# Two graph-attention layers, 16 groups in a software pipeline: next group's statistics and the first attention's tiles set elsewhere in the order

## Chip, cores and metric

One core of a Trainium2 chip. The time is device microseconds of one execution. The kernel before takes 1215.11 us (median of 3 runs, 1213.73 to 1215.54).

## The reference, cut to what matters

`x` is 128 graphs of 64 nodes with 384 features, `adj` a boolean 64x64 matrix for each graph. Two residual layers:

```python
h = relu(layernorm(x))
# layer 0: 12 heads of 32, additive attention
v  = einsum('bnd,ade->bane', h, W); th = tanh(v)
s  = th @ w_src + (th @ w_dst)^T;   s = leaky(s, 0.2); s = where(adj, s, -999)
y  = elu(softmax(s) @ v + b);       g = sigmoid(h @ H_w.T + H_b)
x  = x + g * y + (1 - g) * h
h = relu(layernorm(x))
# layer 1: 6 heads of 64, dot-product attention
q, k, v = h @ Wq + bq, h @ Wk + bk, h @ Wv + bv
x  = x + softmax(q k^T / 8 + mask(adj)) @ v @ Wf + bf
```

## The kernel before, in words

A group is 8 graphs, 512 token rows, held as 4 tiles of 128 rows (`TILES`); there are 16 groups. Nothing of the loop runs on the host: `iterations` writes out 17 rounds, i = 0 to 16. In round i the engines do layer 0 of group i, layer 1 of group j = i - 1, and prepare the normalised input of group i + 1 (`norm0`, `inv_std(0, i + 1)`, `normalise0`, `turn_h0`, `h0_parts`, `h0_lows`). Each engine has its own written order, and semaphores with constant counts tie them together. There is no other scheduler. A dense product in fp32 is made as three products of a high and a low part (`product`, L611 to L613), so a left operand is turned by TensorE into PSUM, copied by ScalarE as the high part, and VectorE makes the low part from the same PSUM bank.

TensorE's order in a round, with the names used below:

- head: four tiles of values (W0) and gate (Hw) of layer 0; then the turns of `th` (L597), of the layer-1 input `p1` (L597), and the small product for source and destination scores (L691), up to the first `Wq` product.
- middle: Q, the layer-0 score blocks (L679), K, V, the masks (L727), the layer-1 scores (L741).
- tail: the turns of the next h0 (`turn_h0`), the turns of the layer-0 probabilities (`turn_probs`, 6 banks), `attend0` of a pair of tiles twice (L775), the turns of the layer-1 probabilities, `attend1` twice (L793), the turns of the layer-1 result (L597, `attn1_low`), and the `Wf` product.

VectorE in the head: `values0(0)` (adds the bias to the first value tile, L911), then `norm0(i + 1)` (four BATCH_NORM_STATS L823 and four BATCH_NORM_AGGREGATE L828, behind a wait for the load of x), then `values0(1)`, the mask, `values0(2)`, `values0(3)`, `hT1l` (L988), the blocks of destination scores (L993); then `softmax0` of four tiles (from L959). In the tail: maxima and differences of the layer-1 scores (L946, L948), `mask1` (L1010), `h0_lows` (L839), `divide0` of four tiles (L888, L890), `divide1` of four (L899, L901), `close(0)`, and the low part of the layer-1 result (L1024), which the `Wf` product waits for.

ScalarE takes `values0_made` of a tile before its tanh (L459), and does `normalise1` (L420, four tiles) between the tanh of tile 1 and that of tile 2. POOL computes the reciprocal deviations (`inv_std`, L364 to L372), adds to x, and waits for VectorE's `gated`. SP loads x of group i + 2 once the store of group j has landed.

PSUM has 8 banks, used in a ring. `RING` lists the 64 uses of a round in order, `job(name, k)` is a use's place, its bank is the place modulo 8, and `take` makes TensorE wait for the reader of the use 8 places before. So a change of TensorE's order changes which reader frees which bank.

Of the kernel before, what the change touches and what calls it, by code (L numbers as in the profile page):

```python
# [8 lines left out]
ALU = mybir.AluOpType  # L9
# [6 lines left out]
P = 128  # L16
# [15 lines left out]
def two_layer_gnn(nc, x, adj, W0, b0, w_src, w_dst, H_w, H_b, Wq, bq, Wk, bk, Wv, bv, Wf, bf, out, d_scratch):  # L32
# [5 lines left out]
    with ExitStack() as ctx:  # L38
# [181 lines left out]
        def jobs(name, layer, signal, n):  # L220
# [14 lines left out]
            + jobs("values1_made", 1, values1_made, 4)  # L235
            + jobs("scores1_shifted", 1, scores1_shifted, 4)
            + jobs("h0_low", NEXT, h0_low, 3)
            + jobs("probs0T_copied", 0, probs0T_copied, 6)
            + jobs("attn0_made", 0, attn0_made, 4)
            + jobs("probs1T_copied", 1, probs1T_copied, 3)  # L240
            + jobs("attn1_made", 1, attn1_made, 4)
            + jobs("attn1_low", 1, attn1_low, 3)
            + jobs("out_made", 1, out_made, 4)
# [4 lines left out]
        def job(name, k):  # L248
            return place[name, k]

        def last_reader(i, at):
# [27 lines left out]
        def _(sp):  # L279
# [28 lines left out]
            def body(i, par):  # L308
                j = i - 1
                if real(i + 1):  # L310
                    load_adj(i + 1, 1 - par)
                if i == 0:
                    load_x(2)
                if real(i):
                    sp.wait_ge(values0_made, TILES * (i + 1))
                    if real(j):
                        sp.wait_ge(attn0_full, 2 * i)
                    else:
                        sp.wait_ge(ones_made, 3)
                    for g in range(2):  # L320
                        for o in range(2):
                            sp.dma_start(V0[64 * o:64 * o + 64, g, o].rearrange("p t k e -> p (t k) e")[:, :, 0:E0],
                                         v_tok[64 * g:64 * g + 64].rearrange("p t (k o e) -> p (t k) o e", o=2, e=E0)[:, :, o])\
                                .then_inc(values0_spread, 16)
                if real(j):
                    sp.wait_ge(values1_made, TILES * (j + 1))
                    if real(j - 1):
                        sp.wait_ge(attn1_full, 2 * j)
                    for g in range(2):
                        for o in range(2):  # L330
                            sp.dma_start(V1[64 * o:64 * o + 64, g].rearrange("p t k e -> p (t k) e")[:, :, 0:E1],
                                         v_tok[64 * g:64 * g + 64].rearrange("p t (k o e) -> p (t k) o e", o=2, e=E1)[:, :, o])\
                                .then_inc(values1_spread, 16)
                if real(j):
                    sp.wait_ge(out_made, (j + 1) * TILES)
                    sp.dma_start(out_v[j], x_in[:, j % 3]).then_inc(out_stored, 16)
                    if real(i + 2):
                        sp.wait_ge(out_stored, 16 * (j + 1))
                        load_x(i + 2)
# [6 lines left out]
        def _(pool):  # L346
# [36 lines left out]
            def body(i, par):  # L383
                j = i - 1
                if real(j):
                    inv_std(1, j)
                if real(i + 1):
                    inv_std(0, i + 1)
                if real(j):
# [3 lines left out]
                if real(i):  # L393
                    pool.wait_ge(h0_made, TILES * (i + 1))
                    for t in range(TILES):
                        pool.tensor_tensor(x_in[:, i % 3, t], x_in[:, i % 3, t], h0[:, par, t], ALU.add).then_inc(x_plus_h, 1)  # L396
                    pool.wait_ge(x_plus_h, TILES * (i + 1))
                    for t in range(TILES):
                        pool.wait_ge(gated, TILES * i + t + 1)
                        pool.tensor_tensor(x_in[:, i % 3, t], x_in[:, i % 3, t], ee[:, t], ALU.subtract).then_inc(x2_made, 1)  # L400
# [5 lines left out]
        def _(act):  # L406
# [27 lines left out]
            for c in range(C):  # L434
                act.activation(wh["Hw"][:, c, :], ps[:, 1 + c, 0:D], ACT.Copy).then_inc(w_high, 1)
            act.wait_ge(w_loaded["W0"], 16 * C)
# [14 lines left out]
            def body(i, par):  # L451
# [13 lines left out]
                def copy_q(c):  # L465
                    if real(j):
                        if c == 0 and real(j - 1):
                            act.wait_ge(scores1_full, 2 * j)
                        if c == 0 and real(i - 1):
                            act.wait_ge(attn0_full, 2 * i)  # L470
                        act.wait_ge(q_full, C * j + c + 1)
# [45 lines left out]
                if real(i):  # L517
                    if real(j):
                        act.wait_ge(attn0_full, 2 * i)
                    else:  # L520
                        act.wait_ge(w_low, C)
# [9 lines left out]
                if real(i):  # L531
# [7 lines left out]
                    act.activation(src_rows[:], sd, ACT.Identity, scale=is_dst_src[:, 1:2], bias=is_dst_src[:, 0:1]).then_inc(srcdst_copied, 1)  # L539
                if real(i + 1):  # L540
                    normalise0(i + 1, 1 - par)
                copy_q(0)
# [5 lines left out]
                leaky(3)  # L548
                exp0(0)
                if real(i):  # L550
                    for t in range(TILES):
# [7 lines left out]
                exp0(3)  # L559
                if real(i + 1):  # L560
                    h0_parts(i + 1)
                if real(i):
# [13 lines left out]
                exp1(3)  # L576
                exp_elu(0)
                exp_elu(1)
                if real(j):
                    for c in range(3):  # L580
                        act.wait_ge(probs1_turned, 3 * j + c + 1)
                        act.activation(KT[:, c], ps[:, job("probs1T_copied", c) % BANKS], ACT.Copy).then_inc(probs1T_copied, 1)
                exp_elu(2)
                exp_elu(3)
                if real(j):
                    act.wait_ge(values1_full, TILES * (j + 1))
                    for c in range(C):
                        act.wait_ge(attn1_turned, C * j + c + 1)
                        act.activation(hT1h[:, c], ps[:, job("attn1_low", c) % BANKS], ACT.Copy).then_inc(attn1_high, 1)

            iterations(act, body)
# [3 lines left out]
        def _(pe):  # L595
# [23 lines left out]
            for c in range(C):  # L619
                for f in range(C):  # L620
                    mm = turn(ps[:, 1 + c, f * P:(f + 1) * P], staged["Hw"][:, f, c * P:(c + 1) * P])
                mm.then_inc(hw_turned, 1)
# [20 lines left out]
            def body(i, par):  # L643
# [119 lines left out]

                def attend0(pair):

                    pe.wait_ge(values0_spread, 64 * (i + 1))
                    pe.wait_ge(probs0T_copied, 6 * i + 3 * pair + 3)
                    for t in (2 * pair, 2 * pair + 1):
                        take(i, job("attn0_made", t))
                        bank = ps[:, job("attn0_made", t) % BANKS, 0:HEADS0 * (E0 + 1)].rearrange("p (k o e) -> p k o e", o=2, e=E0 + 1)  # L770
                        for k in range(PAIRS0):
                            q, at = divmod(t * PAIRS0 + k, 4)
                            turned = QT[:, q] if q < 3 else thT[:, q - 3]
                            for g in range(2):
                                mm = pe.matmul(bank[g * N:(g + 1) * N, k], turned[:, at * P + g * N:at * P + (g + 1) * N],  # L775
                                               V0[:, g, :, t, k], start=True, stop=True, skip_group_check=True)
                    mm.then_inc(attn0_full, 1)

                def attend1(pair):
# [15 lines left out]
                    mm.then_inc(attn1_full, 1)  # L795

                if real(i + 1):
                    turn_h0(i, i + 1, 1 - par)
                if real(i):
                    turn_probs("probs0T_copied", probs0_made, probs0_turned, z, PAIRS0, i, 6)  # L800
                    attend0(0)
                    attend0(1)
                if real(j):
                    turn_probs("probs1T_copied", probs1_made, probs1_turned, p1, PAIRS1, j, 3)
                    attend1(0)
                    attend1(1)
                    pe.wait_ge(attn1_made, TILES * (j + 1))
                    turn_tokens("attn1_low", attn1_made, attn1_turned, lambda t, c: p1[:, t, c * P:(c + 1) * P], i, j)
# [11 lines left out]
        def _(dve):  # L820
# [23 lines left out]
            for c in range(C):  # L844
                dve.wait_ge(w_high, c + 1)
                dve.tensor_tensor(wl["Hw"][:, c, :], ps[:, 1 + c, 0:D], wh["Hw"][:, c, :].bitcast(F32), ALU.subtract)\
                    .then_inc(small_ready, 1)
# [33 lines left out]
            def body(i, par):  # L881
                j = i - 1

                def divide0(t):
                    if real(i):
                        v = ps[:, job("attn0_made", t) % BANKS, 0:HEADS0 * (E0 + 1)].rearrange("p (h e) -> p h e", e=E0 + 1)
                        dve.wait_ge(attn0_full, 2 * i + t // 2 + 1)
                        dve.reciprocal(rs0[:, t], v[:, :, E0]).then_inc(inv0_made, 1)  # L888
# [85 lines left out]
                values0(0)  # L974
                if real(i + 1):
                    norm0(i + 1)
                values0(1)
# [12 lines left out]
                if real(i):  # L990
# [4 lines left out]
                                      is_head[:].unsqueeze(1).unsqueeze(3).broadcast_to((P, 2, HEADS0, N)), ALU.mult)\  # L995
                        .then_inc(dst_blocks_made, 1)
                softmax0(0)
                softmax0(1)
# [13 lines left out]
                if real(i + 1):  # L1012
                    h0_lows(i + 1)
                for t in range(TILES):
                    divide0(t)
                if real(j):
                    dve.wait_ge(probs1_turned, 3 * (j + 1))
                for q in range(TILES):
                    divide1(q)
                close(0)  # L1020
                if real(j):
# [42 lines left out]
```

## Time and profile before

| what | value |
|---|---|
| median of 3 runs | 1215.11 us |
| the profiled execution, its own time | 1212.82 us |
| its span | 1211.0 us |
| TensorE matmul busy | 1034.0 us (85%) |
| VectorE busy | 770.3 us (64%) |
| ScalarE busy | 588.1 us (49%) |
| POOL busy | 258.8 us (21%) |
| mean granted TensorE clock | 0.933 |

The busy share is a mean over stages: where TensorE has work queued it is at 100%, and the rest are waits at the same places of every round. The timeline rows below give the start and the length of a merged run of instructions, both in microseconds, and in brackets how long the engine sat idle before it and whose result ended that. The first W product of a round starts it: round 2 at 140.04 us, round 9 at 650.58, round 10 at 723.88, round 15 at 1089.35. A merged run's length ends with its last instruction's end, and instructions overlap a little, so times from start to start are used where rows allow it.

### The profile page before, as it was taken

How to read it: one execution, taken by the hardware profiler on the slowest of the kernel's cores; microseconds unless marked ns; L12 is line 12 of the kernel's file. 1: busy time of each engine (PE TensorE's matmuls, PEld its weight loads, DVE VectorE, ACT ScalarE, POOL GpSimd, SP SyncE). 2: the span in 40 equal slices, each digit the busy share in tenths (PEclk: the TensorE clock that was granted, in tenths of full speed). 3: DMA queues.
4: the chain of work that ended last, by engine and by line, in shares of the span. 5: the costliest groups of instructions: out<-in, count | busy, mean ns of one | idle time of the engine just before them, and what ended most of it. 6: DMA issues, size and time to landing. Idle time of an engine off the chain costs nothing.

```text
span 1211.0 us, 24852 instructions
## 1 busy us (share of the span) xinstructions
PE 1034.0 (85%) x10153; PEld 894.5 (74%) x10153; DVE 770.3 (64%) x1456; ACT 588.1 (49%) x1126; POOL 258.8 (21%) x338
## 2 busy tenths in 40 slices
PE   4779888897988879888898888979888799889876
PEld 4577868777786777868777686768867778688765
DVE  6567658476583757757476583866847476585734
ACT  5646274461735626364361744626455262745421
POOL 2140131402213031130401313022130401313020
PEclk9779999899898999999899898999989899999988
DMA  8211121411113132121311213122231311213102
GB/s 211 28 27 27 53 29 28 79 28 54 27 28 80 28 72 26 38 52 28 80 28 54 27 28 80 28 62 24 49 54 28 80 28 55 27 29 53 28 26 53
DMA packets 183653, 56.41 MB, mean 47 GB/s; under 512 B 164979, under 2 KB 183541, under 8 KB 183541
## 3 DMA queue, kind: packets, MB, share of 16 engines
q1 hardware_dynamic: 183540, 54.83, 23.4%
q8 instruction: 81, 1.33, 0.4%
q14 instruction: 32, 0.25, 0.1%
HBM read 17.06 MB, written 12.58 MB: 24 GB/s over the span
## 4 chain that ended last, share of the span: by engine, by line
PE 52%; DVE 26%; DMA 9%; issue 6%; ACT 5%; SPq 1%; POOL 0%; DVEq 0%; ACTq 0%; POOLq 0%
PE ps L611 10%; PE ps L597 10%; PE ps L613 10%; PE ps L612 10%; DMA x_in<-in_x_dram 5%; DVE stats L823 4%; PE ps L775 4%; PE ps L679 4%; DMA out_dram<-x_in 4%; DVE x L923 3%; DVE p L948 3%; DVE ee L920 3%; DVE mx L946 3%; DVE p L901 3%; ACT p L420 2%
## 5 line engine op out<-in xcount | busy, mean ns | idle before, releaser
L400 POOL TENSOR_TENSOR x_in<-x_in,ee 128x384 f32<-128x384 f32 x64 | 69.3, 1083 | 695.9 <-DVE ee L926 695.9
L459 ACT ACTIVATE th<-ps 128x384 f32<-128x384 f32 x64 | 31.3, 489 | 307.7 <-DVE v_tok L911 307.7
L597 PE MATMUL ps<-ident,p 128*128 128x128 f32 x576 | 96.1, 330 | 47.3 <-DVE p L901 36.9
L823 DVE BATCH_NORM_STATS2 stats<-x_in 128x6 f32<-128x384 f32 x128 | 63.2, 547 | 107.1 <-DMA x_in<-in_x_dram 107.1
L597 PEld LDWEIGHTS ps<-ident,p 128*128 128x128 f32 x576 | 83.7, 172 | 52.1 <-DVE p L901 39.1
L597 PE MATMUL ps<-ident,th 128*128 128x128 f32 x192 | 48.5, 391 | 78.5 <-ACT th L459 78.5
L959 DVE COPY_PREDICATED_SCALAR z<-not_adj,masked 128x768 f32 x64 | 69.3, 1083 | 66.3 <-ACT z L491 66.3
L988 DVE TENSOR_TENSOR hT1l<-ps,hT1h 128x512 fp32r<-128x512 f32 x48 | 31.7, 689 | 110.0 <-ACT hT1h L530 109.1
L597 PEld LDWEIGHTS ps<-ident,th 128*128 128x128 f32 x192 | 34.1, 197 | 89.6 <-ACT th L459 89.5
L497 ACT ACTIVATE z<-z 128x768 f32<-128x768 f32 x64 | 54.6, 853 | 62.0 <-DVE z L964 60.5
L611 PE MATMUL ps<-Wf_hi,hT1h 128*128 128x384 f32 x192 | 70.7, 368 | 5.5 <-DVE hT1l L1024 5.3
L611 PE MATMUL ps<-W_hi,hT0h 128*128 128x384 f32 x192 | 65.3, 340 | 7.8 <-DVE b_plus L864 6.8
L396 POOL TENSOR_TENSOR x_in<-x_in,h 128x384 f32<-128x384 f32 x64 | 68.6, 1102 | 0.0
L392 POOL TENSOR_TENSOR x_in<-x_in,bf_row 128x384 f32<-128x384 f32 x64 | 61.9, 999 | 30.2 <-ACT p L420 30.2
L597 PE MATMUL ps<-ident,z 128*128 128x128 f32 x384 | 57.1, 289 | 12.7 <-DVE p L948 6.8
L612 PE MATMUL ps<-Wf_lo,hT1h 128*128 128x384 f32 x192 | 67.6, 352 | 0.0
L613 PE MATMUL ps<-Wf_hi,hT1l 128*128 128x384 f32 x192 | 66.8, 348 | 0.0
L491 ACT ACTIVATE z<-ps 128x384 f32<-128x384 f32 x128 | 52.5, 497 | 28.1 <-PE ps L679 28.1
L613 PE MATMUL ps<-W_hi,hT0l 128*128 128x384 f32 x192 | 65.1, 339 | 0.0
L612 PE MATMUL ps<-W_lo,hT0h 128*128 128x384 f32 x192 | 64.9, 338 | 0.0
L611 PE MATMUL ps<-Hw_hi,hT0h 128*128 128x384 f32 x192 | 64.8, 338 | 0.0
L613 PE MATMUL ps<-Hw_hi,hT0l 128*128 128x384 f32 x192 | 64.7, 337 | 0.0
(129 smaller groups left out, 2860.8 us busy)
## 6 DMA issues: line engine op xcount, KB each, us to landing
V<-v_tok SPq DMA_DIRECT2D x128, 192.0 KB, 4.7
x_in<-in_x_dram SPq DMA_DIRECT2D x16, 768.0 KB, 4.6
out_dram<-x_in SPq DMA_DIRECT2D x16, 768.0 KB, 3.6
x<-in_L_gnn_H_w_dram SPq DMA_DIRECT2D x1, 576.0 KB, 5.9
QT<-in_L_gnn_W_dram SPq DMA_DIRECT2D x3, 192.0 KB, 6.7
thT<-in_L_gnn_Wq_dram SPq DMA_DIRECT2D x1, 576.0 KB, 6.1
z<-in_L_gnn_Wk_dram SPq DMA_DIRECT2D x1, 576.0 KB, 7.2
z<-in_L_gnn_Wv_dram SPq DMA_DIRECT2D x1, 576.0 KB, 8.2
```

Source lines behind the costliest of these rows:

```text
L392: pool.tensor_tensor(x_in[:, j % 3, t], x_in[:, j % 3, t], bf_row[:], ALU.add).then_inc(x2_biased, 1)
L396: pool.tensor_tensor(x_in[:, i % 3, t], x_in[:, i % 3, t], h0[:, par, t], ALU.add).then_inc(x_plus_h, 1)
L400: pool.tensor_tensor(x_in[:, i % 3, t], x_in[:, i % 3, t], ee[:, t], ALU.subtract).then_inc(x2_made, 1)
L491: act.activation(z[:, t, half_of * D:(half_of + 1) * D], ps[:, job("leaky_made", 2 * t + half_of) % BANKS, 0:D], ACT.Prelu, alpha=SLOPE).t ...
L497: act.activation(z[:, t], z[:, t], ACT.Exp).then_inc(probs0_made, 1)
L597: return pe.transpose(dst, src, ident[0:rows, 0:rows])
L611: pe.matmul(dst, left_h(c), right_h(c), start=(c == 0), stop=False)
L612: pe.matmul(dst, left_h(c), right_l(c), start=False, stop=False)
L613: mm = pe.matmul(dst, left_l(c), right_h(c), start=False, stop=(c == C - 1 and not more))
L679: mm = pe.matmul(ps[64 * g:64 * g + 64, job("leaky_made", 2 * t + half_of) % BANKS, 0:D], src_rows[rows, g * N:(g + 1) * N], thT[rows].rea ...
L823: dve.bn_stats(stats[:, layer, t], src).then_inc((stats0, stats1)[layer], 1)
L959: dve.copy_predicated(zt, not_adj[:, t].unsqueeze(1).broadcast_to((P, HEADS0, N)), masked0[:].unsqueeze(2).broadcast_to((P, HEADS0, N))).t ...
```

## The change

VectorE, POOL and ScalarE:

- `norm0(i + 1)` moves from between `values0(0)` and `values0(1)` to behind the destination blocks (L993), in front of `softmax0(0)`.
- POOL's `inv_std(0, i + 1)` moves behind the eight additions to x (`x2_biased`, `x_plus_h`), in front of the waits for `gated`.
- ScalarE's `normalise0(i + 1)` moves from in front of `copy_q(0)` to behind `exp0(0)`; `h0_parts(i + 1)` moves from in front of the copies of the layer-0 probabilities to behind `exp1(3)`; the copies of the turned layer-1 probabilities go in front of `exp_elu(0)`, and the copies of the turned layer-1 result in front of `exp_elu(2)`.

TensorE and the divisions:

- The turns of the layer-0 probabilities come in front of `turn_h0`.
- `attend0` takes one tile, and signals for each tile. Tile 0 comes behind `turn_h0`, tile 1 behind the turns of the layer-1 probabilities, tiles 2 and 3 behind both `attend1`.
- VectorE divides tiles 0 and 1 of layer 0, then all of layer 1, then tiles 2 and 3.
- `RING` follows that order. The counts of `attn0_full` are per tile. The start-up turns of `Hw` use the banks behind those of `h0_low`.

```diff
-            + jobs("probs0T_copied", 0, probs0T_copied, 6)
-            + jobs("attn0_made", 0, attn0_made, 4)
+            + jobs("probs0T_copied", 0, probs0T_copied, 6)
+            + jobs("attn0_made", 0, attn0_made, 4)[0:1]
             + jobs("probs1T_copied", 1, probs1T_copied, 3)
+            + jobs("attn0_made", 0, attn0_made, 4)[1:2]
             + jobs("attn1_made", 1, attn1_made, 4)
+            + jobs("attn0_made", 0, attn0_made, 4)[2:4]
...
@@ gpsimd
-                if real(i + 1):
-                    inv_std(0, i + 1)
...
+                if real(i + 1):
+                    inv_std(0, i + 1)
                 if real(i):
                     pool.wait_ge(x_plus_h, TILES * (i + 1))
...
@@ scalar
-                if real(i + 1):
-                    normalise0(i + 1, 1 - par)
                 copy_q(0)
...
                 exp0(0)
+                if real(i + 1):
+                    normalise0(i + 1, 1 - par)
...
                 exp0(3)
-                if real(i + 1):
-                    h0_parts(i + 1)
...
                 exp1(3)
-                exp_elu(0)
-                exp_elu(1)
+                if real(i + 1):
+                    h0_parts(i + 1)
                 if real(j):
                     for c in range(3):
                         act.wait_ge(probs1_turned, 3 * j + c + 1)
...
-                exp_elu(2)
-                exp_elu(3)
+                exp_elu(0)
+                exp_elu(1)
                 if real(j):
                     act.wait_ge(values1_full, TILES * (j + 1))
...
+                exp_elu(2)
+                exp_elu(3)
...
@@ tensor
-                def attend0(pair):
+                def attend0(t):
+                    if real(i):
+                        pe.wait_ge(values0_spread, 64 * (i + 1))
+                        pe.wait_ge(probs0T_copied, 6 * i + ((t + 1) * PAIRS0 - 1) // 4 + 1)
...
+                if real(i):
+                    turn_probs("probs0T_copied", probs0_made, probs0_turned, z, PAIRS0, i, 6)
                 if real(i + 1):
                     turn_h0(i, i + 1, 1 - par)
-                if real(i):
-                    turn_probs("probs0T_copied", probs0_made, probs0_turned, z, PAIRS0, i, 6)
-                    attend0(0)
-                    attend0(1)
+                attend0(0)
                 if real(j):
                     turn_probs("probs1T_copied", probs1_made, probs1_turned, p1, PAIRS1, j, 3)
+                attend0(1)
+                if real(j):
                     attend1(0)
                     attend1(1)
+                attend0(2)
+                attend0(3)
...
@@ vector
                 values0(0)
-                if real(i + 1):
-                    norm0(i + 1)
                 values0(1)
...
+                if real(i + 1):
+                    norm0(i + 1)
                 softmax0(0)
...
-                for t in range(TILES):
-                    divide0(t)
+                divide0(0)
+                divide0(1)
                 if real(j):
                     dve.wait_ge(probs1_turned, 3 * (j + 1))
                 for q in range(TILES):
                     divide1(q)
+                divide0(2)
+                divide0(3)
                 close(0)
```

## Rows read from the trace of the kernel before

**Rows 1.** The page, busy time: us, share, instructions.

```profile
PE 1034.0 (85%) x10153; PEld 894.5 (74%) x10153; DVE 770.3 (64%) x1456; ACT 588.1 (49%) x1126; POOL 258.8 (21%) x338
```

**Rows 2.** The waits, all rounds: us in total, times, longest us.

```profile
DVE stats L823 <- DMA x_in<-in_x_dram: 107.1, 14, 8.2
PE ps L597 <- ACT th L459: 78.5, 42, 3.1
```

**Rows 3.** The timeline of TensorE: starts of rounds 2 and 9, round 9's head.

```profile
140.04 0.34 PE L611 MATMUL ps<-W_hi,hT0h 128*128 128x384 f32 x1
...
644.17 0.41 PE L611 MATMUL ps<-Wf_hi,hT1h 128*128 128x384 f32 x1 [0.81 <-DVE hT1l L1024]
...
650.58 0.34 PE L611 MATMUL ps<-W_hi,hT0h 128*128 128x384 f32 x1
...
663.75 0.27 PE L597 MATMUL ps<-ident,th 128*128 128x128 f32 x1
...
675.70 0.50 PE L611 MATMUL ps<-hT1h,Wq_hi 128*128 128x512 f32 x1
```

**Rows 4.** The timeline of VectorE and POOL in round 9's head.

```profile
655.33 0.55 DVE L911 TENSOR_TENSOR v_tok<-ps,b_plus 128x384 f32<-128x384 f32 x1
663.85 1.94 DVE L823 BATCH_NORM_STATS2 stats<-x_in 128x6 f32<-128x384 f32 x4 [7.97 <-DMA x_in<-in_x_dram]
665.98 0.53 DVE L911 TENSOR_TENSOR v_tok<-ps,b_plus 128x384 f32<-128x384 f32 x1
...
666.76 1.04 POOL L369 TENSOR_TENSOR rstd<-ve,minus_half 128x4 f32<-128x4 f32 x1
```

**Rows 5.** The timeline of TensorE and VectorE in round 15.

```profile
1089.35 0.34 PE L611 MATMUL ps<-W_hi,hT0h 128*128 128x384 f32 x1
...
1106.16 0.47 PE L611 MATMUL ps<-hT1h,Wq_hi 128*128 128x512 f32 x1
...
1113.15 1.09 DVE L959 COPY_PREDICATED_SCALAR z<-not_adj,masked 128x768 f32 x1 [4.28 <-ACT z L491]
...
1130.67 1.30 PE L597 MATMUL ps<-ident,z 128*128 128x128 f32 x8
```

**Rows 6.** The timeline of ScalarE, round 9: the middle's last exponential, then the tail.

```profile
697.01 0.85 ACT L497 ACTIVATE z<-z 128x768 f32<-128x768 f32 x1 [3.80 <-DVE z L964]
...
701.00 1.58 ACT L429 ACTIVATE hT0h<-ps 128x512 fp32r<-128x512 f32 x3 [3.14 <-PE ps L597]
...
706.14 1.00 ACT L502 ACTIVATE p<-p 128x384 f32<-128x384 f32 x2
```

**Rows 7.** The timeline of TensorE in round 9's tail, and round 10's start.

```profile
700.24 1.53 PE L597 MATMUL ps<-ident,h 128*128 128x128 f32 x12
...
714.46 2.32 PE L597 MATMUL ps<-ident,p 128*128 128x128 f32 x12 [2.35 <-DVE p L901]
716.80 0.66 PE L611 MATMUL ps<-Wf_hi,hT1h 128*128 128x384 f32 x1
...
723.88 0.34 PE L611 MATMUL ps<-W_hi,hT0h 128*128 128x384 f32 x1
```

**Rows 8.** The timeline of VectorE in round 9's tail.

```profile
704.12 1.88 DVE L839 TENSOR_TENSOR hT0l<-ps,hT0h 128x512 fp32r<-128x512 f32 x3
707.20 0.23 DVE L888 RECIPROCAL rs<-ps 128x12 f32<-128x12 f32 x1 [1.21 <-PE ps L775]
...
711.54 0.20 DVE L899 RECIPROCAL rs<-ps 128x6 f32<-128x6 f32 x1 [1.32 <-PE ps L793]
...
715.97 1.32 DVE L1024 TENSOR_TENSOR hT1l<-ps,hT1h 128x512 fp32r<-128x512 f32 x2
```

**Rows 9.** Stretches: us, TensorE busy (instructions), granted clock, DMA share, GB/s.

```profile
644.00:651.00 7.00, 6.83 (x39) 1.00 0.00 0
671.00:675.70 4.70, 4.70 (x45) 0.67 1.20 115
716.80:723.90 7.10, 7.10 (x37) 0.88 0.00 1
```

More of the change, by code:

```diff
@@ L249, in job, with hw_bank @@
             return place[name, k]
+        def hw_bank(c):
+            return (job("h0_low", C - 1) + 1 + c) % BANKS
         def last_reader(i, at):
@@ L316, in body @@
                     if real(j):
-                        sp.wait_ge(attn0_full, 2 * i)
+                        sp.wait_ge(attn0_full, TILES * i)
                     else:
@@ L434, in _ @@
             for c in range(C):
-                act.activation(wh["Hw"][:, c, :], ps[:, 1 + c, 0:D], ACT.Copy).then_inc(w_high, 1)
+                act.activation(wh["Hw"][:, c, :], ps[:, hw_bank(c), 0:D], ACT.Copy).then_inc(w_high, 1)
             act.wait_ge(w_loaded["W0"], 16 * C)
@@ L469, in copy_q @@
                         if c == 0 and real(i - 1):
-                            act.wait_ge(attn0_full, 2 * i)
+                            act.wait_ge(attn0_full, TILES * i)
                         act.wait_ge(q_full, C * j + c + 1)
@@ L518, in body @@
                     if real(j):
-                        act.wait_ge(attn0_full, 2 * i)
+                        act.wait_ge(attn0_full, TILES * i)
                     else:
@@ L620, in _ @@
                 for f in range(C):
-                    mm = turn(ps[:, 1 + c, f * P:(f + 1) * P], staged["Hw"][:, f, c * P:(c + 1) * P])
+                    mm = turn(ps[:, hw_bank(c), f * P:(f + 1) * P], staged["Hw"][:, f, c * P:(c + 1) * P])
                 mm.then_inc(hw_turned, 1)
@@ L762, in turn_probs @@
                         mm.then_inc(done, 1)
-                def attend0(pair):
-                    pe.wait_ge(values0_spread, 64 * (i + 1))
-                    pe.wait_ge(probs0T_copied, 6 * i + 3 * pair + 3)
-                    for t in (2 * pair, 2 * pair + 1):
+                def attend0(t):
+                    if real(i):
+                        pe.wait_ge(values0_spread, 64 * (i + 1))
+                        pe.wait_ge(probs0T_copied, 6 * i + ((t + 1) * PAIRS0 - 1) // 4 + 1)
                         take(i, job("attn0_made", t))
@@ L776, in attend0 @@
                                                V0[:, g, :, t, k], start=True, stop=True, skip_group_check=True)
-                    mm.then_inc(attn0_full, 1)
+                        mm.then_inc(attn0_full, 1)
                 def attend1(pair):
@@ L795, in attend1 @@
                     mm.then_inc(attn1_full, 1)
+                if real(i):
+                    turn_probs("probs0T_copied", probs0_made, probs0_turned, z, PAIRS0, i, 6)
                 if real(i + 1):
                     turn_h0(i, i + 1, 1 - par)
-                if real(i):
-                    turn_probs("probs0T_copied", probs0_made, probs0_turned, z, PAIRS0, i, 6)
-                    attend0(0)
-                    attend0(1)
+                attend0(0)
                 if real(j):
                     turn_probs("probs1T_copied", probs1_made, probs1_turned, p1, PAIRS1, j, 3)
+                attend0(1)
+                if real(j):
                     attend1(0)
                     attend1(1)
+                attend0(2)
+                attend0(3)
+                if real(j):
                     pe.wait_ge(attn1_made, TILES * (j + 1))
@@ L845, in _ @@
                 dve.wait_ge(w_high, c + 1)
-                dve.tensor_tensor(wl["Hw"][:, c, :], ps[:, 1 + c, 0:D], wh["Hw"][:, c, :].bitcast(F32), ALU.subtract)\
+                dve.tensor_tensor(wl["Hw"][:, c, :], ps[:, hw_bank(c), 0:D], wh["Hw"][:, c, :].bitcast(F32), ALU.subtract)\
                     .then_inc(small_ready, 1)
@@ L886, in divide0 @@
                         v = ps[:, job("attn0_made", t) % BANKS, 0:HEADS0 * (E0 + 1)].rearrange("p (h e) -> p h e", e=E0 + 1)
-                        dve.wait_ge(attn0_full, 2 * i + t // 2 + 1)
+                        dve.wait_ge(attn0_full, TILES * i + t + 1)
                         dve.reciprocal(rs0[:, t], v[:, :, E0]).then_inc(inv0_made, 1)
```

## The prediction

> **What bounds the kernel now.** I read the page first. TensorE is busy 85% of the span and nothing else is above 64% [rows 1], so the question is where TensorE's missing part lies. The view of waits answers it: it waited 42 times, 78.5 us, for ScalarE's tanh (L459), which is three times in each of rounds 1 to 14. Beside it VectorE waited 107.1 us for the load of x in front of BATCH_NORM_STATS, 14 times, one of them at the start [rows 2].
>
> The timeline of round 9 shows the chain. `values0(0)` starts at 655.33, then VectorE stands at `norm0` for 7.97 us until x lands at 663.85. The statistics take 2.1 us, and `values0(1)` starts at 665.98 [rows 4]. ScalarE's tanh of tiles 1 to 3 waits behind that, and TensorE, which has had the th turns at hand since 663.75, gets to its first Wq product at 675.70 [rows 3]. From the round's start at 650.58 that is 25.12 us. Afterwards its clock is still low: 0.67 granted between 671.0 and 675.7 [rows 9]. So the load of x sits on TensorE's path, through VectorE's written order alone.
>
> Round 15 is the comparison to look for, since there group 16 does not exist and `norm0` is left out. There the round's start to Wq is 1106.16 - 1089.35 = 16.81 us [rows 5]. Everything else of the head is in it.
>
> The round's other idle place is the tail: TensorE waits 2.35 us for `divide1` before it turns the layer-1 result [rows 7].
>
> **The head.** Moving `norm0` behind L993 should make every head of rounds 2 to 14 like round 15's: 16.81 us. What hides it in its new place: VectorE there sat idle 4.28 us before `softmax0(0)` [rows 5], and `norm0` takes 2.13 us (663.85 to 665.98) [rows 4]. Without that cover it would delay the softmax by 2.1 us, and that still has a wait of its own behind it (ScalarE was idle 3.80 us before the last exponential [rows 6], because VectorE waits for V in between). x lands 13.3 us after the round's start (663.85 against 650.58), `norm0` now comes some 19.5 us after it (16.81 to Wq, then L988 and L993), so the wait for x has 6 us to spare, and 2 us of cover more. SP's store and load are issued at the same distance from the start. The four V DMAs are issued when `values0(3)` is done, which is now earlier, and no new DMA stands in front of them.
>
> POOL's `inv_std(0, i + 1)` is four small instructions, 1.04 us the longest [rows 4], about 2 us together. It waits behind eight additions that it used to precede, and they are done by then. `normalise0` is wanted only by `turn_h0` in the tail. On ScalarE it now delays three of the four exponentials and the K copies by 2.5 us (estimate: as `normalise1`'s and its own four activations), and the 3.80 us idle before the last exponential takes it in [rows 6]. I cost all of this at nothing. The middle stays at 1130.67 - 1106.16 = 24.51 us [rows 5].
>
> **The tail, walked through in round 9's times.** The order of TensorE's work changes, its amount does not. The tail begins at 700.24 [rows 7].
>
> - ScalarE starts at 701.00 as before. The h0 copies were first, 1.58 us less an overlap, say 1.5 [rows 6]. Now three copies, two exponentials, three copies and two exponentials come first, so the h0 copies begin at 701.00 + (706.14 - 701.00 - 1.5) + 0.9 = 705.5.
> - VectorE was at `h0_lows` at 704.12 [rows 8]. Now it stands there until the first high part is copied: 705.5 + 0.6 = 706.1 (both 0.6 from a third of 1.58 and the handover). This is a new wait of 2.0 us.
> - What VectorE does from there to the low part of the layer-1 result, at 715.97, is the same work in another order: h0_lows, eight divisions, `close(0)`. Its 11.85 us held two waits, 1.21 and 1.32 us [rows 8], for `attend0` and `attend1`. In the new order both inputs are there in time: the first tile of layer 0 is ready near 705.8, the first pair of layer 1 near 709.2, where VectorE asks at 708.0 + 1.5 = 709.5. So 9.3 us of work from 706.1 on, ending at 715.4.
> - Of the gain of 2.5 us in waits, then, 2.0 are given back in the new wait. `divide1` does end earlier, near 712.3, and TensorE starts the turns at 712.4 instead of 714.46. But its next wait is for L1024, which comes behind `divide0(2)`, `divide0(3)` and `close(0)`. The `Wf` product starts 0.83 us behind L1024 (716.80 - 715.97), so at 716.2 instead of 716.80. That is 15.94 us after the tail's start.
>
> TensorE's wait of 2.35 us thus becomes one of about 1.2 us before the turns and one of 2.4 us between them and `Wf`.
>
> **The clock in the tail.** In round 8's tail `Wf` took 6.41 us to the next round (644.17 to 650.58) at a granted clock of 1.00; in round 9's it took 7.08 (716.80 to 723.88) at 0.88 [rows 3, 7, 9]. There the turns ran first after the wait and took 2.32 us, some 0.8 more than their 1.53 in the turns of h0 at full clock [rows 7]. So a clock that has fallen costs about 1.5 us in this place, and before, more than half of that lay in the turns, which ended before VectorE was done. Now the wait is directly in front of `Wf`, and all of it is on the path. Bounds: nothing (as round 8), or 1.5 us in every round. Both cases occur, so I take 1.0. `Wf` is then 7.4 us and the tail 15.94 + 7.4 = 23.35 us, against 23.64 in round 9 (700.24 to 723.88). The tail's own gain is near zero.
>
> [...]
>
> **Sum.** Rounds 2 to 14 last 1089.35 - 140.04 = 949.31 us, 73.02 each [rows 3, 5]. A round after: 16.81 + 24.51 + 23.35 = 64.67. Saved 8.35 in each, 13 times: 108.6 us. In round 1 x is loaded early and only the 2.1 us of `norm0` itself stand in the way: about 2. Rounds 0, 15 and 16 I take as unchanged; in round 0 the turns, the copies and the low parts only change places behind a softmax that sets the pace (bounds: 1 us either way). Together 110.6. The profiled execution took 1212.8, so 1102.2; the median of the runs lies 2.3 above the profiled one, so 1104.5 us, as I predict it: 1104.
>
> **Rivals.**
>
> 1. The clock falls in front of `Wf` every time, at its full price or a little more, and the new order in the tail costs more than it gives: 23.85 to 24.9 us for a tail. For it: two waits close together with 1.4 us of work between. Against: one wait of the same 2.35 us left round 8's clock alone. Price 0.5 to 1.5 us in each of 14 rounds: 1111 to 1126. Chance 0.13.
> 2. The tail gains. The clock does not fall, or VectorE reaches L1024 sooner since the h0 copies come sooner: a tail of 21.9 to 22.6 us. Against: ScalarE's queue in front of `h0_parts` is fixed work of 4.5 us. Time 1084 to 1094. Chance 0.14.
> 3. The wait for x only moves: x lands later than `norm0`'s new place and holds up the softmax, with `scores` and the probabilities' turns behind it. It takes a landing more than 8 us later than 13.3 us after the round's start, and nothing in SP's order makes it later. A miss of 3 us in each of 13 rounds would give 1143. Chance 0.01.
> 4. Slower. TensorE stays at 1.2 GHz from the wait before `Wf` through `Wf` and the next head's four tiles. At the half rate 6.4 + 13.2 us of work become twice as long, 19.6 us more in a round, and the change loses from 8.3 us on. At the full price it gives 1104 + 13 x 18.6 = 1346 us. Against it: in round 9 the clock, at 0.67 just before, was back for the whole Wq stretch, and after the wait of 2.35 us `Wf` averaged 0.88 and not 0.5 [rows 9]. Chance 0.02.
>
> My forecast, the heads as round 15's and the tail within 0.5 us of what it was, has 0.70: 1098 to 1111. The range for eight in ten takes in most of rivals 1 and 2: 1087 to 1122. A difference under 0.2% is what a measurement of this kernel cannot tell from no change. Faster by more: cases 1, 2, 3 and the forecast, 0.97; within: 0.01; slower: 0.02.
>
> **What would show it.** In the changed kernel: VectorE's wait for x in front of L823 gone (from 107.1 to the start's own), and TensorE's three waits for L459 in a round gone; Wq 16.8 us after the round's first W product in rounds 2 to 14; granted clock 1.00 through the head. In the tail a new wait of VectorE of about 2 us at L839 for ScalarE's hT0h, the turns of the layer-1 result near 12.1 us after the tail's start, and a TensorE wait of about 2.4 us for L1024, with `Wf` starting 15.9 us after the tail's start. The step I trust least is the tail's clock. The prediction is wrong if the distance from the tail's start to `Wf` is over 17 us or under 15, or if Wq comes later than 17.5 us.

## The result, and the profile after

The changed kernel takes 1101.09 us (median of 4 runs, 1099.41 to 1104.05) against 1215.25 us (median of 4 runs of the kernel before beside it): a ratio of 0.9066, 95% interval 0.9045 to 0.9086. The profiled execution took 1099.41 us, its span is 1097.5 us. The forecast was 1104 us, with a range of 1087 to 1122.

The page's first lines, of after:

```profile
span 1097.5 us, 24884 instructions
...
PE 995.7 (91%) x10153; PEld 872.2 (79%) x10153; DVE 766.0 (70%) x1456; ACT 583.3 (53%) x1126; POOL 253.7 (23%) x338
```

TensorE does the same 10153 matmuls in 38 us less of busy time, since more of them run at the higher clock (mean granted 0.965, before 0.933). The rest of the 113.5 us by which the span shrank is waiting that is gone. The view of waits, after (us in total, times, longest), answers to [rows 2]:

```profile
PE ps L617 <- DVE hT1l L1035: 34.1, 15, 2.3
DVE hT0l L848 <- ACT hT0h L435: 32.4, 15, 4.1
PE ps L603 <- DVE p L910: 14.2, 15, 1.8
DVE stats L832 <- DMA x_in<-in_x_dram: 5.4, 1, 5.4
PE ps L603 <- ACT th L465: 0.8, 2, 0.4
```

The wait for x is left once, at the start of the kernel, and TensorE's wait for tanh fell from 78.5 to 0.8 us. In their place stand the two that the walk through the tail foresaw: VectorE for the h0 copy (about 2.0 us a round) and TensorE for the low part in front of `Wf` (2.27 us, 15 times).

Round 9 of after, TensorE's timeline (start and length in us, idle before in brackets), with the starts of rounds 2, 9, 10 and 15:

```profile
134.99 0.34 PE L617 MATMUL ps<-W_hi,hT0h 128*128 128x384 f32 x1
...
587.99 0.34 PE L617 MATMUL ps<-W_hi,hT0h 128*128 128x384 f32 x1
...
601.16 1.47 PE L603 MATMUL ps<-ident,th 128*128 128x128 f32 x12
...
604.80 0.47 PE L617 MATMUL ps<-hT1h,Wq_hi 128*128 128x512 f32 x1
...
629.32 2.84 PE L603 MATMUL ps<-ident,z 128*128 128x128 f32 x24
...
641.47 1.53 PE L603 MATMUL ps<-ident,p 128*128 128x128 f32 x12 [0.93 <-DVE p L910]
645.27 0.41 PE L617 MATMUL ps<-Wf_hi,hT1h 128*128 128x384 f32 x1 [2.27 <-DVE hT1l L1035]
645.52 0.33 PE L618 MATMUL ps<-Wf_lo,hT1h 128*128 128x384 f32 x1
...
653.18 0.34 PE L617 MATMUL ps<-W_hi,hT0h 128*128 128x384 f32 x1
...
977.44 0.34 PE L617 MATMUL ps<-W_hi,hT0h 128*128 128x384 f32 x1
```

Read it against [rows 3], [rows 5] and [rows 7]. From the round's start to Wq it is now 604.80 - 587.99 = 16.81 us, to the hundredth what round 15 of before had. The turns of th are one run of 12 without a gap. The middle is 24.52 us. `Wf` starts 645.27 - 629.32 = 15.95 us behind the tail's start (forecast 15.94). Rounds 2 to 14 last 977.44 - 134.99 = 842.45 us, 64.80 each, against a forecast of 64.67 and 73.02 before.

VectorE in round 9's head and tail:

```profile
605.76 1.75 DVE L1000 TENSOR_TENSOR thT<-dst_rows,is_head 128x1536 f32<-128x1536 f32 x1
607.43 1.93 DVE L832 BATCH_NORM_STATS2 stats<-x_in 128x6 f32<-128x384 f32 x4
609.28 0.36 DVE L837 BATCH_NORM_AGGREGATE mv<-stats 128x2 f32<-128x6 f32 x4
611.79 1.10 DVE L968 COPY_PREDICATED_SCALAR z<-not_adj,masked 128x768 f32 x1 [2.15 <-ACT z L497]
...
635.29 1.89 DVE L848 TENSOR_TENSOR hT0l<-ps,hT0h 128x512 fp32r<-128x512 f32 x3 [2.02 <-ACT hT0h L435]
...
642.79 0.55 DVE L929 SCALAR_TENSOR_TENSOR ee<-ee,x 128x384 f32<-128x384 f32 x1
...
644.44 1.28 DVE L1035 TENSOR_TENSOR hT1l<-ps,hT1h 128x512 fp32r<-128x512 f32 x2
```

The statistics lie in what was idle time: of the 4.28 us in front of the softmax [rows 5], 2.15 are left. `close(0)` begins at 642.79. ScalarE has begun to copy the turned layer-1 result at 642.22 (three copies in 1.57 us), so about then the first low part could be made; it has to wait for `close(0)` until 644.44.

The stretches of round 9, after (us, TensorE busy, granted clock, DMA share, GB/s): head, its end, middle, tail, `Wf`, and the `Wf` of round 8.

```profile
588.00:601.40 13.40, 13.40 (x80) 1.00 0.39 122
601.40:604.80 3.40, 3.34 (x49) 1.00 0.92 133
604.80:629.40 24.60, 24.60 (x223) 1.00 0.14 16
629.40:645.30 15.90, 12.29 (x253) 1.00 0.30 49
645.30:653.20 7.90, 7.90 (x37) 0.78 0.00 1
581.50:588.00 6.50, 6.42 (x37) 1.00 0.00 0
```

The head's end had 0.67 before [rows 9] and has 1.00. `Wf` is the only one of these stretches whose clock falls, and not in every round: in round 8 it ran 6.4 us at 1.00, in round 9 7.9 us at 0.78. The fall comes after the wait, not in it: the second product of `Wf` still takes 0.33 us, those from 646.06 to 648.94 take 0.53 us, and from 649.5 on the granted clock is 1.00 again. By the timeline, from the first `Wf` product to the last one's end, it is 6.57 us in four of rounds 1 to 14 and 7.96 to 8.07 in ten.

### The profile page after: what moved, and what is told of

Read it like the earlier page. It is cut to its first block, busy times and chain, and to the rows that moved or that the text cites. A ratio compares the mean times of both kernels' runs of the same rounds, so it can differ in the third digit from the quotient of the medians.

```text
span 1097.5 us, 24884 instructions
## 1 busy us (share of the span) xinstructions
PE 995.7 (91%) x10153; PEld 872.2 (79%) x10153; DVE 766.0 (70%) x1456; ACT 583.3 (53%) x1126; POOL 253.7 (23%) x338
## 4 chain that ended last, share of the span: by engine, by line
PE 71%; DVE 16%; ACT 8%; issue 4%; DMA 0%; POOL 0%; ACTq 0%; DVEq 0%; POOLq 0%
PE ps L617 20%; PE ps L619 18%; PE ps L618 18%; PE ps L603 5%; PE ps L685 4%; DVE p L910 3%; DVE hT0l L848 3%; ACT QT L572 2%; ACT p L508 2%; PE ps L747 2%; DVE x L899 2%; ACT thT L578 2%; DVE x L932 1%; PE ps L697 1%; DVE ee L929 1%
## 5 line engine op out<-in xcount | busy, mean ns | idle before, releaser
L617 PE MATMUL ps<-Wf_hi,hT1h 128*128 128x384 f32 x192 | 73.3, 382 | 34.1 <-DVE hT1l L1035 34.1
L603 PE MATMUL ps<-ident,p 128*128 128x128 f32 x576 | 77.1, 284 | 25.7 <-DVE p L910 14.2
L920 DVE TENSOR_TENSOR v_tok<-ps,b_plus 128x384 f32<-128x384 f32 x64 | 35.0, 553 | 92.5 <-PE ps L619 92.3
L603 PEld LDWEIGHTS ps<-ident,p 128*128 128x128 f32 x576 | 65.4, 145 | 30.8 <-DVE p L910 16.3
L617 PEld LDWEIGHTS ps<-Wf_hi,hT1h 128*128 128x128 f32 x192 | 41.3, 215 | 39.0 <-issue 37.4
L618 PE MATMUL ps<-Wf_lo,hT1h 128*128 128x384 f32 x192 | 71.1, 370 | 0.0
L619 PE MATMUL ps<-Wf_hi,hT1l 128*128 128x384 f32 x192 | 70.8, 369 | 0.0
L503 ACT ACTIVATE z<-z 128x768 f32<-128x768 f32 x64 | 54.5, 853 | 28.1 <-DVE z L973 28.0
L947 DVE TENSOR_TENSOR v_tok<-ps,bv_row 128x384 f32<-128x384 f32 x64 | 34.1, 553 | 45.1 <-PE ps L619 45.1
L618 PE MATMUL ps<-Hw_lo,hT0h 128*128 128x384 f32 x192 | 65.4, 340 | 0.0
```

The lines of the kernel that those rows point to most:

```text
L503: act.activation(z[:, t], z[:, t], ACT.Exp).then_inc(probs0_made, 1)
L603: return pe.transpose(dst, src, ident[0:rows, 0:rows])
L617: pe.matmul(dst, left_h(c), right_h(c), start=(c == 0), stop=False)
L618: pe.matmul(dst, left_h(c), right_l(c), start=False, stop=False)
L619: mm = pe.matmul(dst, left_l(c), right_h(c), start=False, stop=(c == C - 1 and not more))
L920: dve.tensor_tensor(v_tok[:, t].rearrange("p (h e) -> p h e", e=E0), ps[:, job("th_made", t) % BANKS, 0:D].rearrange("p (h e) -> p h e", e ...
```

## The experiments

All times below are medians with the ratio to the kernel before, measured on the same chip, and its 95% interval.

**The two halves, one at a time.** `e1` keeps the changed tail and puts the statistics back:

```diff
                 values0(0)
+                if real(i + 1):
+                    norm0(i + 1)
                 values0(1)
...
-                if real(i + 1):
-                    norm0(i + 1)
                 softmax0(0)
```

and likewise `inv_std(0, i + 1)` in front of the additions and `normalise0(i + 1)` in front of `copy_q(0)`.

> Only the order of the tail is changed (turns, attend0 by tiles, divisions, copies, ring); norm0, inv_std(0, i + 1) and normalise0 stay where the kernel before has them. My theory: the heads keep their stall, which hangs on the load of x and through it on VectorE's end of the tail. That end comes 0.6 us sooner in each round (Wf started 15.94 us behind the tail's start in my walk, 16.5 before), and what the clock costs in front of Wf is hidden by the stall of the next head. So 14 x 0.6 = 8 us less: about 1207 us. Rival: the tail's order is worth nothing by itself or costs its clock: 1215 to 1225.

1200.1 us, 0.9884 (0.9861 to 0.9907). That is 7 us faster than my theory's 1207, and the rival is out. The wait for x stays (108.5 us, 14 times) and so do TensorE's 42 waits for tanh. `e2` is the reverse: the kernel before with only the statistics moved.

> Only norm0, inv_std(0, i + 1) and normalise0 are moved; the tail is as in the kernel before. My theory: the whole gain is here. Heads of 16.8 us as in the changed kernel, tails of about 23.3 us as before: 1215 - 13 x 8.3 - 2 = about 1105 us. Wq comes 16.8 us behind the round's first W product. Rival: the two parts need each other (the statistics in their new place hold the softmax up in the old tail's timing): 1120 us or more.

1104.23 us, 0.9097 (0.9081 to 0.9113), and Wq 16.81 us behind the start in rounds 2 to 14. So nearly the whole gain is the statistics' place: 110 us of 114, by itself.

Why the tail alone gave more than 8 us is seen when a round is cut at the points of the chain through the load. Worked out from both timelines, us, means over rounds 2 to 14 (L1024 and L1035 are the same low part):

```
                              before   e1     difference x 13
low part -> store of x         12.22  12.10    1.6
store -> x landed               8.26   8.37   -1.3
x landed -> Wq                 12.26  12.01    3.3
Wq -> next low part            40.30  39.68    8.1
```

The four parts are a cut of the round, 73.0 us before, so that they add up to it says nothing of slack. What shows the ring (low part, last additions, store, load, statistics, tanh, turns, Wq) is that its links wait for each other in every one of these rounds: the load is issued 0.02 us after the store has landed, VectorE stands idle until x lands, TensorE until tanh is done. `e1` then gives the proof: a low part that comes 0.6 us sooner shortens the round by at least as much. The last row is my 0.6 us a round. The third is the clock: from the start of the last turn of `th` to Wq it took 3.37 us on the mean before and 3.12 in `e1`, since less of that stretch ran at the low clock. The four rows make 11.7 us of the 15.9 by which the span shrank. Most of the rest is in round 1 (72.2 to 69.8 us) and in the last tail (some 1.5 us), where no h0 copy has to be waited for; I had left both out.

**Which engine's move matters.** `e3` leaves `norm0` where the change puts it and puts POOL's and ScalarE's parts back:

```diff
@@ gpsimd
                     inv_std(1, j)
+                if real(i + 1):
+                    inv_std(0, i + 1)
...
-                if real(i + 1):
-                    inv_std(0, i + 1)
...
@@ scalar
+                if real(i + 1):
+                    normalise0(i + 1, 1 - par)
                 copy_q(0)
...
                 exp0(0)
-                if real(i + 1):
-                    normalise0(i + 1, 1 - par)
```

> The changed kernel with VectorE's norm0 in its new place, but POOL's inv_std(0, i + 1) and ScalarE's normalise0 put back to their old places. My theory: ScalarE now stands in front of copy_q(0) until norm0 (ending about 5 us behind Wq) and POOL's four instructions (2 us) are done, then spends 2.4 us on normalise0, so the first leaky copy comes some 4.5 us later than in the changed kernel, and TensorE waits about 3 to 4 us for banks in front of the second blocks: 1101 + 14 x 3.5 = about 1150 us. Rival: only VectorE's order mattered, and ScalarE's and POOL's places are free: 1101 us.

1157.01 us, 0.9525 (0.9503 to 0.9547): 56 us dearer than the changed kernel, 7 us more than my theory gave, so the moves that I cost at nothing are free only in their new place. ScalarE and TensorE, round 9 of `e3`:

```profile
646.42 2.50 ACT L418 ACTIVATE h<-x_in,shift,rstd 128x384 f32<-128x384 f32 x4 [6.04 <-POOL shift L377]
648.83 1.24 ACT L478 ACTIVATE QT<-ps,bq_col 128x512 f32<-128x512 f32 x2
...
650.49 1.52 PE L685 MATMUL ps<-thT,src_rows 32*64 32x384 f32 x16 [2.75 <-ACT z L497]
```

ScalarE stands 6.04 us for the shift, then Q's copy is late, and the second block of scores finds its banks taken. The middle takes 28.90 us in this round against 24.52. The wait of 2.75 us is not all of it: behind it, between 652.1 and 655.5, the granted clock is 0.50. Rounds 2 to 14 take 68.49 us each, 3.7 more than in the changed kernel and near my 3.5; round 1 takes 7 us more, and there my theory was short. The wait for the new statistics had only been handed on, from VectorE to ScalarE and from there to TensorE.

**How much room norm0 has.** `e7` and `e8` set it earlier in the changed kernel (both also take it out of its place in front of `softmax0(0)`):

```diff
@@ e7
+                if real(i + 1):
+                    norm0(i + 1)
                 if real(j):
                     for c in range(C):
                         dve.wait_ge(h1_high, C * j + c + 1)
...
@@ e8
+                if real(i + 1):
+                    norm0(i + 1)
                 values0(3)
```

> The changed kernel with norm0 in front of hT1l (L995) instead of behind the destination blocks. My theory: x lands some 13.3 us behind the round's first W product, values0(3) is done by 12.2, and hT1l is due at 16.0. The statistics take 2.1 us from 13.3 to 15.4 and are just in time: 1100 to 1104 us, Wq still 16.8 us behind the start. Rival: any place of norm0 in front of TensorE's first Wq costs its 2.1 us: 1101 + 13 x 2.1 = 1128.

> The changed kernel with norm0 in front of values0(3). My theory: the round hangs on the load again. x lands about 20.3 us behind the low part of the tail (12.1 to the store, 8.2 for store and load), then 2.1 us of statistics, 0.5 for values0(3), 0.5 for its tanh, and some 4.2 us to Wq, 28 us in all against 24.0 to 25.5 in the changed kernel: 2.5 to 3.5 us more a round in 13 rounds, 1133 to 1147 us. Rival: what costs in the kernel before is that three tanhs pile up behind the wait, and one alone costs little: under 1115.

`e7` took 1100.9 us, 0.9067 (0.9047 to 0.9086), the same as the changed kernel. `e8` took 1141.63 us, 0.9403 (0.9387 to 0.942). One instruction of 0.5 us in VectorE's order lies between the two. VectorE in round 9 of `e7`, then the waits of `e8`:

```profile
601.13 0.56 DVE L920 TENSOR_TENSOR v_tok<-ps,b_plus 128x384 f32<-128x384 f32 x1 [2.74 <-PE ps L619]
601.61 1.93 DVE L832 BATCH_NORM_STATS2 stats<-x_in 128x6 f32<-128x384 f32 x4
603.46 0.36 DVE L837 BATCH_NORM_AGGREGATE mv<-stats 128x2 f32<-128x6 f32 x4
605.47 1.89 DVE L997 TENSOR_TENSOR hT1l<-ps,hT1h 128x512 fp32r<-128x512 f32 x3 [1.65 <-ACT hT1h L536]
```

```profile
DVE stats L832 <- DMA x_in<-in_x_dram: 61.6, 14, 5.4
PE ps L603 <- ACT th L465: 37.2, 15, 3.7
```

In this round of `e7` x has landed before the statistics' place is reached, and they end 1.65 us before `hT1l` can start. In five of rounds 2 to 14 VectorE does wait for x there, up to 1.5 us, and Wq comes 16.81 us behind the start all the same: a wait for a load costs nothing as long as it ends before something else does. In `e8` the wait for x is shorter than before (61.6 us in all), but what is queued behind it is the last tile's tanh, for which TensorE waits (37.2 us), and the ring over the load closes again: 67.8 to 68.9 us a round against 63.7 to 65.2.

**The clock in front of Wf.** `e5` fills the wait with work that nobody reads:

```diff
                     turn_tokens("attn1_low", attn1_made, attn1_turned, lambda t, c: p1[:, t, c * P:(c + 1) * P], i, j)
+                    take(i, job("out_made", 0))
+                    for n in range(18):
+                        turn(ps[:, job("out_made", 0) % BANKS, 0:P], ident[:])
```

> The changed kernel with 18 turns of the identity, which nobody reads, set between the turns of the layer-1 result and Wf: 2.1 us of TensorE work at full clock, in a wait of 2.27 us. My theory: the Wf of 8.05 us in 10 of 14 rounds, against 6.57 in the others, is the clock, which falls in that wait. With the wait filled Wf takes 6.57 everywhere and starts at the same place: 10 x 1.48 = 15 us less, about 1086 us. Rival: Wf is slow for another reason (operands, banks, VectorE reading the same banks): unchanged at 1101, or slower by what the filler overruns.

1087.73 us, 0.8957 (0.8944 to 0.8971). TensorE, round 9 of `e5`:

```profile
634.34 1.53 PE L603 MATMUL ps<-ident,p 128*128 128x128 f32 x12 [0.94 <-DVE p L913]
635.70 2.13 PE L603 MATMUL ps<-ident 128*128 128x128 f32 x18
638.14 0.41 PE L617 MATMUL ps<-Wf_hi,hT1h 128*128 128x384 f32 x1 [0.31 <-DVE hT1l L1038]
```

`Wf` starts where it did (15.97 us behind the tail's start, against 15.95) and takes 6.58 us in every round. The granted clock over rounds 2 to 14 is 1.00 (0.98 in the changed kernel). 2.1 us of useless turns in each round make the kernel 13 us faster, and the operands, banks and readers of `Wf` are the same as before. So the extra 1.4 to 1.5 us are the clock, and without the idle time in front of `Wf` they are gone.

The filler is not free everywhere. Rounds 2 to 14 together are 14.4 us shorter (828.09 us against 842.45), as my theory has it. In the last round, where no layer 0 work is left and `Wf` has no such wait, the turns stand in its way: from the start of round 15 to the end the kernel takes 122.4 us instead of 120.1.

The idle time alone does not bring the fall either. `e8` has the same two waits in its tail, 0.94 and 2.28 us, and its `Wf` takes 6.57 us in all of rounds 1 to 14. There the clock falls in the head instead, in every one of rounds 2 to 14, behind TensorE's wait for the last tanh: 0.51 granted between 628.8 and 632.3 us in round 9, after a wait of 2.70 us. `e1` has the same two waits as well and a slow `Wf` in two rounds of 14. What decides in which of several waits the clock falls stays open.

**The wait in front of Wf itself.** `e4` moves one more call:

```diff
                 divide0(2)
                 divide0(3)
-                close(0)
                 if real(j):
                     for c in range(C):
                         dve.wait_ge(attn1_high, C * j + c + 1)
...
+                close(0)
                 close(1)
```

> The changed kernel with one more move: VectorE's close(0) comes behind the three low parts of the layer-1 result instead of in front of them. My theory: in the changed kernel Wf waits 2.27 us for VectorE alone, which does divide0(2), divide0(3) and close(0) (1.65 us) first. Without close(0) Wf starts 1.3 to 1.65 us sooner, and the wait left, 0.6 to 1 us, is short enough for the clock to stay at full, so the Wf of about 8.05 us that 10 of 14 rounds show becomes 6.57: 2.4 to 2.7 us in each round, 1062 to 1068 us. The next head has room for a VectorE that is 1.65 us later than TensorE. Rival: VectorE's total sets the round, and the next head waits for values0(0) instead: 1095 to 1101 us.

1064.56 us, 0.8769 (0.8755 to 0.8784): as my theory had it, 36 us less than the changed kernel, and the fastest version here. Round 10's tail and the next head in `e4`, TensorE first, then VectorE:

```profile
684.12 1.53 PE L603 MATMUL ps<-ident,p 128*128 128x128 f32 x12 [0.94 <-DVE p L910]
686.35 0.41 PE L617 MATMUL ps<-Wf_hi,hT1h 128*128 128x384 f32 x1 [0.69 <-DVE hT1l L1034]
```

```profile
699.87 1.01 DVE L920 TENSOR_TENSOR v_tok<-ps,b_plus 128x384 f32<-128x384 f32 x2
700.80 0.28 DVE L989 TENSOR_SCALAR not_adj<-adj_in 128x256 uint8<-128x256 uint8 x1
701.10 0.56 DVE L920 TENSOR_TENSOR v_tok<-ps,b_plus 128x384 f32<-128x384 f32 x1
704.40 0.56 DVE L920 TENSOR_TENSOR v_tok<-ps,b_plus 128x384 f32<-128x384 f32 x1 [2.73 <-PE ps L619]
```

The wait in front of `Wf` is 0.69 us instead of 2.27, and `Wf` takes 6.57 us in every round. VectorE is later against TensorE in the next head and takes two value tiles at once at 699.87, but it is waiting for TensorE again by the fourth. 13 rounds of 62.1 us instead of 64.8 make 35 of the 36. Of these 35 the earlier start of `Wf`, 1.58 us a round, makes 20.5, and the clock, 1.00 over rounds 2 to 14 here too, the other 14, as much as the filler gave in the same rounds.

`e6` makes the same move in the old tail:

> The statistics moved, the old order of the tail, and close(0) behind the three low parts. My theory: in the old tail Wf waits for a chain that does not pass through close(0): all eight divisions, the turns 14.2 us behind the tail's start, ScalarE's first copy, and then the low part, which could start at most 0.1 us sooner than it does. So it gives at most 0.1 us a round: 1102 to 1105, as with the statistics alone, where the same move is worth 36 us in the new tail. Rival: close(0) costs 1.65 us wherever it stands in front of the low parts: about 1080.

1107.01 us, 0.9115 (0.9099 to 0.9131): no gain over the statistics alone (1104.23, on another chip), and 2 us outside what I expected. `Wf` starts 0.12 us sooner at best; with that, every one of rounds 2 to 14 lost clock in the turns or `Wf` (turns 2.04 to 2.82 us instead of 1.53, `Wf` 7.0 to 7.4), where `e2` had five rounds at full clock. How many rounds keep it changes from one execution to the next: the repeat of `e2` below, `f2`, had two.

**What the tail's order is worth beside the moved statistics.** Both kernels again on one chip, in five rounds:

> The changed kernel again, beside the statistics alone and on the same chip. What the tail's new order is worth once the statistics are moved: its own part of 0.6 us a round in 14 rounds and about 1.5 us in the last tail make 10 us, less what the clock takes back in Wf. My theory: 3 us sooner than the statistics alone (about 1101 against 1104), since the clock takes most of it. Rival: the two are equal within 0.1%, or the 10 us show whole.

> The statistics alone again, with the old tail, beside the changed kernel on the same chip: about 1104 us, 3 us more than the changed kernel, in my theory; equal to it in the rival.

1101.15 us, 0.9081 (0.9067 to 0.9094), against 1104.97 us, 0.9109 (0.9094 to 0.9123). A difference of 3.8 us, with intervals that just touch; the first pair, `e2` and the result, was measured on two chips and differs by 3 us. The traces say where it lies. Rounds 2 to 14 take 842.5 us in `f1` and 843.4 in `f2`, so in the steady rounds the new tail is worth 0.9 us in all. Round 1 is 1.8 us shorter, and what follows the start of round 15 1.7 us.

## Why the prediction was right

The time came out 3 us below the forecast, and the step-by-step account holds. The 3 us themselves come of mis-sized terms that partly cancel (last point):

- **The head** is 16.81 us in rounds 2 to 14, as taken over from round 15. `e2` shows that moving the statistics is nearly the whole of the gain, 110 us of 114, and `e7` beside `e8` that it is the load standing in front of the value tiles that cost it, not the 2.1 us of the statistics.
- **The cover** was there. VectorE's idle time in front of the softmax went from 4.28 to 2.15 us, ScalarE's waits for the softmax's differences (L503) from 60.5 us in all to 28.0, the middle stayed at 24.5. I put x's room at 6 us and 2 of cover. `e7` set `norm0` 7 us sooner in the round at no cost: it starts 12.1 us behind the round's start (601.61 and 589.49), where it stood 19.4 us behind it. "I cost all of this at nothing" was right for the places together; `e3` shows that without the other two moves half of the gain would have been given back.
- **The tail's walk** gave 15.94 us to `Wf`; measured 15.95. The turns start 12.15 us behind the tail's start (forecast 12.1 to 12.2), the new wait of VectorE is 2.02 us (2.0), TensorE's waits in front of the turns and in front of `Wf` are 0.93 (1.2) and 2.27 us (2.4).
- **The clock** I took as 1.0 us on the mean, between 0 and 1.5. It is 1.4 to 1.5 us in 10 of 14 rounds, about 1.0 on the mean, and 1.1 in rounds 2 to 14. The value was a choice between two cases that the trace before shows, not a derivation; that it fell so near is partly luck, and `e8` and `e1` show the same waits in front of `Wf` at a price of nothing in most rounds. (Round 8 of before, my case of a wait that left the clock alone, had waited 2.50 us there, not 2.35.) `e5` settles that the extra time is the clock and that it goes when the wait is filled. My first rival would have had it in every round. It fell in every round of `e6`, in ten of fourteen here, and in none of `e4`, where the waits are 0.94 and 0.69 us. The Trainium skill ("TensorE: Matmul & The Clock Gate", section "HAM oscillation — how this bites in real kernels") describes a loop whose DMA waits, some 3 to 5 us each, put the clock back in every repetition. Here waits of 2.3 us did so, in every round of `e6` and in part of the rounds elsewhere.
- **Mis-sized terms.** By the two profiled executions the span shrank by 113.5 us, where I had 110.6. Rounds 2 to 14 saved 106.9 us, not 108.6: 64.80 us each instead of 64.67, nearly all of it the clock in `Wf`. Round 1 saved 5.4 us (72.22 to 66.79), not 2: 4.2 in its head, where its tanhs no longer pile up behind the statistics, and most of the rest in its `Wf`, which ran at full clock. From the start of round 15 to the end it saved 1.6, which I had taken as nothing, and round 1 began 0.4 us later. The misses go both ways, and the 3 us are what is left of them.

What I did not see is that the tail's order was one call from being worth ten times as much. I had written that `Wf`'s low part "comes behind `divide0(2)`, `divide0(3)` and `close(0)`" and drew no conclusion from it.

## What to carry to other kernels

When a wait for a transfer sits in the middle of an engine's written order, look for an iteration in the same trace in which that instruction is missing: its length is the price, measured. Then move every link of the chain that hangs on the wait (statistics, the small arithmetic on the second engine, the consumer on the third), for one link left in its old place waits in its turn. After such a move read again which instruction the busy engine waits for, and ask for every call in front of it whether it is on that engine's path. Here one such call, 1.65 us long, cost 36 us, about 14 of them through the clock.

## What the runs showed of the hardware

TensorE's clock fell behind a wait of 2.3 us in some rounds and not in others of the same kernel, with the same work on both sides: 0.78 and 1.00 granted over `Wf` in rounds 9 and 8. The same wait with the same work around it was followed by a slow `Wf` in ten rounds of 14 in the changed kernel, in two in `e1` and in none in `e8`, where the clock fell elsewhere in the round. Where the waits were 0.94 and 0.69 us with 1.5 us of turns between them (`e4`), it stayed at 1.00 over rounds 2 to 14. Work without use, 2.1 us of it in a wait of 2.27 us, kept it at 1.00 as well and gave 14 us back in 13 rounds; where there was no wait, in the last round, it cost 2 us.
